# The rows of a prepared group normalised by ScalarE instead of VectorE

## What is computed

```
xn = (x - mean) / sqrt(var + 1e-5)
zxbcdt = xn @ in_proj_w.T                          # gate z, x, B, C, time step dt
xBC = silu(conv_b + sum_k conv_w[:, k] * xBC[t - 3 + k])
h_t = exp(dt * A) * h_(t-1) + dt * B_t x_t         # by chunks in the kernel
y = (C_t h_t + D_skip * x_t) * silu(z)
mamba = (y * rsqrt(mean(y * y) + 1e-5) * norm_w) @ out_proj_w.T
moe = sum over the top 2 experts of p_e * (silu(xn @ gate_e) * (xn @ up_e)) @ down_e
out = x + mamba + moe
```

## Time and profile before

| what | value |
|---|---|
| median of 3 runs | 727.1 us (726.68 to 730.82) |
| profiled execution | 727.78 us, of which the span is 726.0 us |
| TensorE matmul (PE) | 644.9 us busy, 89% |
| VectorE (DVE) | 509.1 us busy, 70% |
| ScalarE (ACT) | 373.9 us busy, 51% |
| GpSimd (POOL) | 316.3 us busy, 44% |

### The profile page before, as it was taken

The page is one execution under the profiler, slowest core; times in us unless marked ns, Lnnn a source line. Parts: engine busy times, 40 slices in busy tenths (PEclk is TensorE's granted clock), DMA queues, the critical chain, the costliest instruction groups (busy, mean ns, idle before and its releaser), DMA issues.

```text
span 726.0 us, 12653 instructions
## 1 busy us (share of the span) xinstructions
PE 644.9 (89%) x4189; PEld 530.0 (73%) x4190; DVE 509.1 (70%) x1116; ACT 373.9 (51%) x787; POOL 316.3 (44%) x223
## 2 busy tenths in 40 slices
PE   4867899999999999999999999888478999999992
PEld 3757769778786777867977877564347889889981
DVE  4965976887887697788798798878866644434430
ACT  3653973754656467276375463647035644444441
POOL 1110144544452553525454425255363565665642
PEclk9968999999999999999999999999778999999996
DMA  8940112230430420403223203093277667676663
GB/s 253 332 142 29 58 61 79 97 117 30 145 118 22 154 107 12 145 32 116 99 78 117 100 18 117 1 273 105 76 207 206 113 121 141 116 132 128 116 101 43
DMA packets 32051, 80.91 MB, mean 111 GB/s; under 512 B 4801, under 2 KB 10049, under 8 KB 29825
## 3 DMA queue, kind: packets, MB, share of 16 engines
q1 hardware_dynamic: 22176, 55.22, 23.2%
q0 software_dynamic: 9056, 21.50, 16.4%
q10 hardware_dynamic: 768, 3.54, 1.6%
HBM read 60.45 MB, written 19.79 MB: 111 GB/s over the span
## 4 chain that ended last, share of the span: by engine, by line
PE 54%; DVE 13%; issue 11%; DMA 8%; ACT 6%; POOL 5%; SPq 1%; DVEq 0%; POOLq 0%; ACTq 0%
PE pi L1415 15%; PE pg L1605 11%; PE po L1454 8%; PE pd L1618 7%; DMA e<-cs_d 7%; DVE xs L917 3%; PE px L1588 2%; PE py L1492 2%; PE py L1499 2%; ACT m L647 2%; PE pxb L1572 2%; POOL y L511 1%; POOL ysq L478 1%; DVE y L1197 1%; PE phs L1628 1%
## 5 line engine op out<-in xcount | busy, mean ns | idle before, releaser
L1415 PE MATMUL pi<-xh,whl 128*128 128x256 f32 x1152 | 169.6, 291 | 5.3 <-DVE zs L923 2.8
L1415 PEld LDWEIGHTS pi<-xh,whl 128*128 128x128 f32 x1152 | 150.6, 194 | 8.6 <-issue 5.4
L917 DVE SCALAR_TENSOR_TENSOR xs<-raw,conv_w,xs 128x256 f32<-128x256 f32 x240 | 110.3, 525 | 14.3 <-ACT xs L622 14.3
L1454 PE MATMUL po<-wo,y 128*128 128x512 f32 x256 | 114.7, 601 | 2.2 <-DVE cbm L1220 1.5
L1415 PE MATMUL pi<-xl,whl 128*128 128x256 f32 x576 | 93.3, 285 | 0.0
L1454 PEld LDWEIGHTS po<-wo,y 128*128 128x128 f32 x256 | 48.1, 193 | 57.2 <-issue 55.3
L531 POOL DMA_INDIRECT out<-yo,idx x39 | 63.0, 1617 | 55.6 <-ACT yo L777 29.8
L1415 PEld LDWEIGHTS pi<-xl,whl 128*128 128x128 f32 x576 | 80.1, 192 | 0.0
L647 ACT ACTIVATE m<-m,cs_tok 128x128 f32<-128x128 f32 x256 | 79.6, 388 | 0.5
L1605 PE MATMUL pg<-ew,xgh 128*128 x312 | 66.1, 355 | 0.0
L506 POOL TENSOR_TENSOR carry<-carry,cd 128x1024 f32<-128x1024 f32 x15 | 29.0, 1934 | 84.2 <-PE py L1492 84.1
(11 more groups left out here) (203 smaller groups left out, 1180.0 us busy)
## 6 DMA issues: line engine op xcount, KB each, us to landing
m<-cs_d SPq DMA_DIRECT2D x16, 1024.0 KB, 5.6
e<-cs_d SPq DMA_DIRECT2D x32, 256.0 KB, 4.9
w_as_read<-in_w_in SPq DMA_DIRECT2D x9, 512.0 KB, 8.2
res<-in_x SPq DMA_DIRECT2D x16, 256.0 KB, 2.8
out<-o SPq DMA_DIRECT2D x16, 256.0 KB
ew<-in_w_gu SPq DMA_DIRECT2D x5, 768.0 KB, 8.9
xin<-in_x SPq DMA_DIRECT2D x6, 512.0 KB, 3.7
xn_d<-xin SPq DMA_DIRECT2D x6, 512.0 KB, 2.8
```

What stands on the lines that cost most here:

```text
L917: dve.scalar_tensor_tensor(out=xs[par][:, b, :], in0=raw[:, b, k:k + GT], scalar=conv_w[:, b, k:k + 1], in1=xs[par][:, b, :], op0=ALU.mult ...
L1415: mm = pe.matmul(bank[:, hf, :], whl[:, weight(g, n), lo, k, hf * P:(hf + 1) * P], xx[:, k, :], start=k3 == 0, stop=k3 == 11)
L1454: mm = pe.matmul(po[:, :], y[:, b, :], wo[:, b, :], start=b == 0, stop=b == XB - 1)
```

## The change

From the third group on, VectorE's `normalise` no longer touches the rows. It works out the shift `-mean * rstdx` for both tiles (128x2, into the scratch column `dif`) and signals `shift_done`. ScalarE waits for it behind the Exp of `e2` and ahead of `decay_factors(t + 1)`, and normalises each tile with one activation, `x * rstdx + shift`. Its two activations now give the counts of `xn_done`. The groups 0 and 1 stay as they were.

```diff
+        shift_done = sem("shift_done")
...
+            def normalise(q):
+                act.wait_ge(shift_done, q - 1)
+                for c in range(2):
+                    xx = x_of(q)[:, c, :]
+                    act.activation(xx, xx, ACT.Identity, bias=dif[:, c:c + 1], scale=rstdx[:, c:c + 1]
+                                   ).then_inc(xn_done, 1)
...
                 act.activation(e2[:, :, :], e2[:, :, :], ACT.Exp).then_inc(e2_done, 1)
                 if c == 1 and prepares:
                     router_rows(g + 2)
+                if c == 0 and prepares:
+                    normalise(g + 2)
                 if more:
                     decay_factors(t + 1)
                     kernel_part(t + 1, 0, 4)
...
             def normalise(q):
                 dve.wait_ge(rstdx_done, q + 1)
                 norm.after()
+                if q >= 2:
+                    dve.scalar_tensor_tensor(out=dif[:, :], in0=mean[:, :], scalar=-1.0, in1=rstdx[:, :],
+                                             op0=ALU.mult, op1=ALU.mult).then_inc(shift_done, 1)
+                    return
                 for c in range(2):
                     xx = x_of(q)[:, c, :]
                     dve.tensor_scalar(xx, xx, mean[:, c:c + 1], rstdx[:, c:c + 1], ALU.subtract, ALU.mult
```

## The result

The changed kernel takes 735.92 us (median of 4 runs, 734.22 to 739.46), the kernel before 726.89 on the same chip (4 runs, 726.17 to 730.82). The ratio is 1.0119, with a 95% interval from 1.0067 to 1.0172: slower by 1.2%. The profiled execution of the changed kernel took 736.42 us with a span of 734.4, which is 8.4 us more span than before.

What follows compares the result with a forecast made beforehand. TensorE, at 89%, was taken to bound the kernel, others counting only where it waits, through ScalarE's queue. Step 0's 1.4 plus 1.03, 1.16, 1.43, 1.43 and 1.03 made 7.5 us over 727.1: 734.6, range 729.5 to 739.5.

Steps and rivals of the forecast that it cites:

- the sign: Whole kernel: slower by over one per cent given 0.54, same 0.43, faster 0.03.
- The activation: ScalarE behind the Exp: 128x512 with scale and bias from columns, about 0.81 us each, the pair delaying the queue 1.43 us.
- The shift operation: VectorE: one 128x2 operation in place of two 128x512 ones, 161 ns.
- The relief: VectorE's queue: about 0.8 us less a group, ending in its wait for ScalarE's first taps, costed at nothing.
- ScalarE's queue carries the delay to `off(1)`: Preparing steps: the added ScalarE time, less slack, delays VectorE's `decayed(0)` and then TensorE's second half of `off`.
- about 6: TensorE's wait for `decayed(0)` at `off(1)`, in five steps: together about 6 us more than now.
- The sum per step: Steps 2, 4, 10: 1.03, 1.16, 1.03 us after slack; steps 6 and 8, already waiting: 1.43 each.
- Step 0's 1.4 us: Step 0: 2.1 us added on ScalarE, 0.7 given back; 1.4 goes through the eight scalings of `wo`.
- Rival (b): Step 8: TensorE's wait grows to 3.1 us and its clock falls, costing up to 3.4 us, 738; chance 0.20.
- The stretch after 444 us only shifted: End of the changed profile, after 444 us: expected to be only shifted.
- (c): Preparing steps: part of the delay is absorbed, +2.5 to +5 us, 729.6 to 732; chance 0.12.
- (d): ScalarE would be waiting anyway for something later than the Exp, so the change doesn't act, 727; chance 0.03.

Runs made afterwards that it cites:

- e1: Kernel before, with VectorE normalising only 16 of the 512 columns of each tile from the third group on: 726.83 us, ratio 0.9983.
- e2: Kernel before plus two spare ScalarE activations of the new form behind the Exp in the preparing steps, VectorE still normalising: 736.07 us, ratio 1.0116.
- e4: Changed kernel with the shift worked out right behind `spread` and ScalarE normalising before it waits for buffer `e2`, step 0 as changed: 729.73 us, ratio 1.0021.
- e11: The changed kernel again, unedited, timed and profiled a second time: 738.0 us, ratio 1.0149 to the kernel before.
- e10: e9 with the load of buffer `e2` placed between the loads of the rows and the decay rows: 727.32 us, ratio 0.9984.
- e5: Kernel before with the load of buffer `e2` issued ahead of the rows and decay rows in steps 2 to 10: 732.49 us, ratio 1.0043.
- e9: e4 with the change only from the fourth group on, so step 0 works as in the kernel before: 730.83 us, ratio 1.0031.
- e3: Changed kernel plus the two spare activations of e2 right behind the normalising ones: 750.68 us, ratio 1.0334.
- e6: Changed kernel with the load of buffer `e2` issued ahead of the rows and decay rows: 742.08 us, ratio 1.0199.
- e7: e6 with the shift worked out right behind `spread`, ScalarE still normalising behind the Exp: 734.04 us, ratio 1.0083.

## Why the prediction was right, and where not

The forecast of 734.6 was 1.3 us under the measured 735.9, and both, with the sign, lie in its range.

**The terms.** The activation, not in the trace of before, was put at 0.81 us and its pair at 1.43 of queue: 802 ns and 1.41 to 1.42. The shift operation was put at 161 ns: 161. The estimate from the Trainium skill ("ScalarE: Activation LUTs", What ACT_TABLE_LOAD costs) was 0.80 and 1.41, and the trace agrees with it a little better than with the forecast's own interpolation. The difference is 0.1 us in the sum.

**The relief brings nothing in steps 2 to 10**: right, shown by e1 and by the wait of 3.34 us. In step 0 it brings 0.6 us, as the forecast had it (0.7).

**ScalarE's queue carries the delay to `off(1)`**: right, shown from both sides, by e2 (the pair alone makes the loss) and e4 (the pair elsewhere does not). TensorE's waits on that line grew by 5.6 us, for which "about 6" stood; the carry wait stayed at 1.0 in steps 2 to 10 where the clock did not fall, and nothing was caught later there.

**The sum per step.** Steps 2, 4 and 10 were put at 1.03, 1.16 and 1.03; in e11 they are 1.06, 1.04 and 1.05. (The forecast had got there by ScalarE's slack behind the Exp; in e11 it is the shift that sets when the pair starts, in step 4 too, where no wait was forecast. The agreement to 0.1 us has some luck in it.) Steps 6 and 8 were put at the full 1.43, since TensorE waits there already; that is a price for a kernel in which `e2` is as late as in that one profile. In e11 step 8 has 27.79, the length of steps 2, 4 and 10. How late `e2` is in step 8 was read as a property of the step; it belongs to the execution. With the first profile of after the five steps are +7.4 us where 6.1 were put, with e11's +5.4.

**Step 0's 1.4 us**: right in its place and nearly in size. ScalarE's queue is 1.2 us longer in both profiles of the changed kernel (12.02 from the Exp to the scalings of `wo`, against 10.81), with 0.48 us of wait for the shift where 0.7 was put; over all profiles it is 1.3. What the forecast did not have is that half clock lies elsewhere in the step from one execution to the next and can hide it, as it did in the first pair of profiles.

**Rival (b), a fall of the clock in step 8**: it happened, with the wait at 1.91 us and not 3.1. The forecast set half clock of 6.8 us at up to 3.4 us; it was 3.4 us long and cost 1.6, of which 0.7 came back at the carry. So the mechanism was right, the place was right, and the price was too high. It is not tied to step 8: in e11 the fall is in step 6. What the text did not see is that it can follow a wait that the kernel before has too: in step 12 TensorE waits 1.81 us at 436.20 before and 1.82 at 442.82 after, at full clock behind the one and at half clock behind the other. "The stretch after 444 us only shifted" failed with that, by 2.3 us in steps 12 and 13. From step 12 on such falls come with and without the loss: between 430 and 510 us e10 and the kernel before have none, e1 has two, and e5 and e9 have three, and steps 12 and 13 of e9 (29.53 and 36.00 us) are as long as those of e11 (29.51 and 36.00). These two steps are 4.4 of the 9.7 us by which the span of e11 exceeds that of the kernel before, and they can't be put down to the change. In steps 2 to 10 it is otherwise. All five profiles with the longer chain behind the Exp have a fall there (after, e2, e3, e6, e11), at waits for `off(1)` of 1.91 to 3.70 us, and only two of the eight others have one (e4 and e7, at 1.65 and 1.97). That speaks for the change making them more frequent in these steps; thirteen profiles do not prove it.

**Rivals (c) and (d)**: neither. Of the forecast's 7.5 us, 6.1 stood in steps 2 to 10, where the first profile has 7.4. The mechanism is the one forecast. That the total came so close has luck in it: in the first pair of profiles step 0's term is hidden, and half clock in steps 8, 12 and 13, most of it not forecast or forecast for another price, took its place.

## What to carry to other kernels

Moving work to a less busy engine is judged by its place in that engine's queue: 1.4 us of work behind a late DMA and ahead of what the next engine waits for cost all of it but the slack, while the same work put into the wait for that DMA cost nothing that could be measured. To price it, follow the queue from the last outside event to TensorE and subtract the slack of each step. An engine whose relief ends in a wait was not the bound, however busy it is. And where the clock moves from one execution to the next, a term of one us is read from the engine's own stretch, not from the length of a step.

## What the runs showed of the hardware

**GpSimd beside VectorE.** The power of 128x2 on GpSimd takes 2.69 us in the kernel before, in step 4, and 0.71 in e4, where VectorE has nothing running. GpSimd's timelines, before and e4:

```profile
188.37 2.69 POOL L461 TENSOR_TENSOR ln<-ln,nhalf 128x2 f32<-128x2 f32 x1 [1.27 <-DVE ln L835]
```

```profile
189.80 0.71 POOL L462 TENSOR_TENSOR ln<-ln,nhalf 128x2 f32<-128x2 f32 x1 [1.28 <-DVE ln L847]
```

In the kernel before VectorE's product of 128x2048 runs from 188.21 to 190.50, and the power ends 0.56 us later. The Trainium skill ("SBUF — State Buffer", SBUF: two separate sides) says that the two engines share a pair of ports, that a VectorE operation with two inputs in SBUF takes it against a GpSimd operation that reads SBUF, and that the one who comes second is blocked for the whole instruction; the product is such an operation, and the two durations agree with it.

**The clock.** TensorE's granted clock fell to 0.50 for 3.4 us behind waits of 1.65 (e4, 320.74), 1.82 and 1.91 us (after, 442.82 and 323.63) and 2.20 (e3, 147.72) on an engine that is 89% busy, and stayed at 1.00 behind waits of 1.81 (before, 436.20) and 2.21 us (e3, 210.28). The fall in step 8 cost TensorE 1.6 us, 0.9 when the carry had given 0.7 back. Steps 12 and 13, which no edit touches, are together 61.1 us in the kernel before and in e10, and 65.5 in e9 and e11.
